# Embedding tower: the look-ups of each sub-block wait for the landing of the pair in front of them

## What is computed

```python
e = stack([tbl_f[ids[:, f]] for f in range(32)], axis=1)     # 1024 x 32 x 64
p, q = e[:, ROW], e[:, COL]                                  # 496 pairs of fields
z = sum(einsum('bpj,ipj->bpi', p, kernel) * q, axis=-1)      # 1024 x 496
h = relu(concat([z, dense_ctx]) @ W_top1 + b_top1)
y = relu(h @ W_top2 + b_top2) @ W_top3
```

## Time and profile before

| | us |
|---|---|
| median of 3 runs (495.70 to 498.19) | 495.96 |
| span of the profiled execution | 412.5 |
| outside the span, by the median | 83.5 |
| PE busy | 403.7 (98%) |
| DVE busy | 298.6 (72%) |
| ACT busy | 259.1 (63%) |
| POOL busy | 231.6 (56%) |

### The profile page before, as it was taken

How to read it: one execution, slowest core, us unless ns; L and a number is a source line. 1 busy time by engine, 2 the same in 40 slices (tenths; PEclk the granted TensorE clock), 3 DMA queues, 4 the chain that set the end, 5 groups by cost and what they waited for, 6 DMA issues and landing times.

```text
span 412.5 us, 10180 instructions
## 1 busy us (share of the span) xinstructions
PE 403.7 (98%) x3421; PEld 254.4 (62%) x3421; DVE 298.6 (72%) x293; ACT 259.1 (63%) x1874; POOL 231.6 (56%) x251
## 2 busy tenths in 40 slices
PE   7889999999999999999999999999999999999997
PEld 5556656667675766666766665666666566654442
DVE  6776887878788887878979798878879888740000
ACT  6476877667577876764796867719978667002221
POOL 6777777777677757776766777677767200000000
PEclk9998999999999999999999999999999999999999
DMA  6665661131281111211211113111311020000000
GB/s 177 210 200 155 191 221 33 27 77 27 37 219 28 29 19 47 61 28 25 63 42 28 25 25 79 24 27 26 79 25 27 15 51 2 2 2 0 2 0 1
DMA packets 18266, 24.31 MB, mean 59 GB/s; under 512 B 6387, under 2 KB 11767, under 8 KB 17958
## 3 DMA queue, kind: packets, MB, share of 16 engines
q1 hardware_dynamic: 10406, 15.64, 13.0%
q0 software_dynamic: 7808, 8.01, 9.7%
HBM read 19.44 MB, written 0.00 MB: 47 GB/s over the span
## 4 chain that ended last, share of the span: by engine, by line
PE 92%; DMA 3%; POOL 3%; issue 1%; ACT 0%
PE u_ps L690 41%; PE z_ps L724 14%; PE u_ps L711 13%; PE z_ps L730 7%; PE u_ps L771 7%; PE t_ps L644 4%; PE u_ps L791 3%; POOL nat L419 3%; DMA nat<-tbl,ids_sb 2%; PE u_ps L697 2%; DMA ids_sb<-ids 1%; PE t_ps L677 0%; PE u_ps L799 0%; ACT y_sb L571 0%
## 5 line engine op out<-in xcount | busy, mean ns | idle before, releaser
L419 POOL DMA_INDIRECT nat<-tbl,ids_sb x244 | 230.5, 945 | 90.7 <-issue 56.6
L607 DVE TENSOR_TENSOR prod<-u_ps,rows 128x1024 f32<-128x1024 f32 x184 | 213.5, 1218 | 56.7 <-PE u_ps L690 56.7
L504 ACT ACTIVATE pass_prod<-pass_prod 128x64 f32<-128x64 f32 x896 | 214.3, 243 | 22.1 <-DVE pass_prod L618 22.1
L690 PE MATMUL u_ps<-rows,k_sb 64*128 64x256 f32 x1472 | 176.2, 387 | 0.0
L504 ACT ACTIVATION_READ_ACCUMULATOR pass_prod<-pass_prod 128x1 f32 x896 | 169.9, 190 | 0.0
L690 PEld LDWEIGHTS u_ps<-rows,k_sb 64*128 64x128 f32 x1472 | 139.0, 188 | 46.0 <-DVE pass_prod L618 13.4
L618 DVE TENSOR_TENSOR pass_prod<-u_ps,nat 128x1024 f32<-128x1024 f32 x56 | 67.2, 1215 | 1.2 <-PE u_ps L711 1.2
L711 PE MATMUL u_ps<-k_sb,rows 64*128 64x256 f32 x448 | 61.5, 394 | 0.6 <-ACT rows L492 0.6
L724 PE MATMUL z_ps<-prod,sel 128*32 128x512 f32 x512 | 61.6, 598 | 0.0
L492 ACT ACTIVATE rows<-t_ps 128x512 f32<-128x512 f32 (+1 forms) x38 | 19.6, 516 | 54.2 <-PE t_ps L644 54.0
L711 PEld LDWEIGHTS u_ps<-k_sb,rows 64*128 64x128 f32 x448 | 40.6, 186 | 14.6 <-DVE prod L607 9.6
(11 more groups left out here) (50 smaller groups left out, 78.9 us busy)
## 6 DMA issues: line engine op xcount, KB each, us to landing
by_self<-rows SPq DMA_DIRECT2D x32, 128.0 KB
nat<-tbl,ids_sb POOLq DMA_INDIRECT x244
k_sb<-kern SPq DMA_DIRECT2D x3, 768.0 KB, 5.6
k_sb<-kern SPq DMA_DIRECT2D x2, 640.0 KB, 5.7
k_sb<-kern SPq DMA_DIRECT2D x1, 1152.0 KB, 5.2
k_sb<-kern SPq DMA_DIRECT2D x2, 512.0 KB
rows<-w SPq DMA_DIRECT2D x1, 1024.0 KB, 6.6
rows<-tbl SPq DMA_DIRECT2D x4, 224.0 KB
```

The costliest lines, as they stand in the source:

```text
L419: pool.indirect_dma_start(nat_of(m, n)[:, h * EMBED:(h + 1) * EMBED], None, tables[f], bass.IndirectOffsetOnAxis(ids_sb[:, col:col + 1], 0 ...
L504: op = nc.scalar.activation(of, of, ACT.Copy, accum_out=z_nat[:, b % 2, s, row:row + 1])
L607: nc.vector.tensor_tensor(to, u, by.unsqueeze(1).to_broadcast([P, 2, 2, SIZE]), ALU.mult).then_inc(prod_ready, 1)
L690: op = nc.tensor.matmul(u[:, h, :], k_sb[part, k_of(d), side, :], rows[part, tile, cols_of(b)], start=True, stop=True)
```

## The change

From tile m = 12 on POOL waits ahead of the first look-up of each sub-block. Ahead of sub-block 0 it waits until all four look-ups of tile m - 1 have landed; ahead of sub-block 1 until both look-ups of sub-block 0 of its own tile have landed. The second look-up of a sub-block follows without a new wait. So at most two look-ups are under way at any time, where before there was no such limit. The waits that were there stay, and no instruction of another engine changes.

```diff
+SPACED = 12
@@ the loop of POOL, for n in range(SUBS)
                 for n in range(SUBS):
+                    if m >= SPACED:
+                        if n == 0:
+                            pool.wait_ge(gathered[(m - 1) % LANES], lane_count(m - 1))
+                        else:
+                            pool.wait_ge(gathered[m % LANES], lane_count(m) - 32)
                     for h in range(2):
                         _, pieces, quads = PLAN.in_front(m, 2 * n + h)
```

## The result

The changed kernel is slower. In the comparison that followed the prediction it took 604.77 us (603.48 to 606.11, 4 runs) against 496.27 us (495.7 to 498.19, 4 runs), a ratio of 1.219 with the interval 1.214 to 1.223. The forecast was 629.5 us with a range of 600 to 656.

What follows compares the result with a forecast made beforehand. PE was taken as the bound; look-up pairs of 3.93 us would delay its last transposes by 131.8 us, and 1.7 us of reduced clock made 133.5 us. Added to 495.96 us this gave 629.5 us, range 600 to 656.

Steps and rivals of the forecast that it cites:

- The mechanism: From m = 16 on POOL's look-ups set the pace: 3.93 us for two instead of 2.64, PE idle about 5 us.
- The step of 1.25 us: On POOL, from first to second look-up issue in a sub-block: 1.25 us, as before, because nothing is waited for between them.
- The landing: From a pair's second look-up issue to its landing: 2.40 us, with 2.20 and 3.01 as ends.
- the case built on it: With a landing of 2.08 us a pair of look-ups takes 3.61 us and the time is near 596 us.
- The release of POOL: From a landing to POOL's next start: 0.28 us in each pair of look-ups, with 0.04 as low end.
- The large loads: Three look-up landings meet two `k_sb` loads and `w1` with `w2`: about 2 us each, 6 us in all.
- The sum: m = 63 lands at 464.4 us; PE's last transposes come 131.8 us later; with 1.7 us of clock, 133.5 us.
- The 83.5 us "outside the span": Time beyond the profiled span of 412.5 us, taken as unchanged and added to the forecast span of 546.0 us.
- The clock: PE runs at reduced clock after idle time; only after the last landing does this count: 1.7 us.
- the rival of the cold PE: Half clock stays on through PE's rounds, 10.7 us of work becomes 21.5; time about 765 us, chance 0.03.
- The waits cost nothing: Rival: look-up pairs with landing and release stay within PE's 2.72 us; time 496 us, chance 0.03.
- the low nor the high landing: Rivals: look-ups land after 2.20 us (584 us with 0.04 release) or 3.01 us (693 us); chance 0.06 each.

Runs made afterwards that it cites:

- after 2: The changed kernel, compared again with the kernel before, and its trace: 588.48 us, ratio 1.426.
- the later before: The kernel before, unchanged, timed again in the second comparison: 412.9 us over 7 runs.

## Why the prediction was right, point by point

*The mechanism.* Right. POOL's time for two look-ups became a closed chain, the lead was used up, and the look-ups set the pace. "About 24 times, some 5 us each", from m = 16 on, was 24 times 5.2 us. That PE waited at m = 13 and 15 already comes from two long steps of POOL at m = 12 and 13, told below.

*The step of 1.25 us* between the two look-ups of a sub-block: 1.24 to 1.25 us.

*The landing.* 2.40 us was taken between bounds of 2.20 and 3.01; it measured 2.40 for the last look-up and 2.45 in the median. Leaning to the low end because the DMA engines were quiet was right. The estimate of 2.08 us by the formula of the Trainium skill ("DMA: Bandwidth & Descriptors", section "Anatomy of one DMA — SWDGE (gpsimd) path") was 0.3 to 0.4 us short of it, and the case built on it, near 596 us, did not come about beside a before of the same speed.

*The release of POOL.* This is the term that was mis-sized. 0.28 us came from the only row in which POOL started on a landing, and it holds where the DMA carries the wait. It was applied to both waits. Ahead of sub-block 0 the landing is waited for by a separate instruction, and the release there is 0.75 us. That is 0.47 us more for each of 52 tiles, 24 us. The typical tile is 8.45 us and not 7.86, 31 us over 52 tiles; the 6 us that the release does not explain are landings a little above 2.40. The order listing in the front part shows the difference (`gathered4,transposed` against `gathered5` in the last place), but I had not read it as a price. The two kernels with the wait written first confirm the term.

*The large loads.* 6 us were taken. The distance from the landing of m = 11 at about 49.6 us to that of m = 63 at 504.7 is 455.1 us; 52 tiles of 8.45 are 439.4, so 15.7 us lie in single long steps. The three landings that the prediction named are there: 5.50 us at m = 12 and 6.27 at m = 13, beside the last `k_sb` loads, and 6.39 at m = 22, just behind the issue of `w1` and `w2` at 141.5 and 142.2 us. Against the usual steps they cost 9.5 us and not 6. The first of them in POOL's timeline of after 2:

```profile
51.57 0.94 POOL L425 DMA_INDIRECT nat<-tbl,ids_sb  x1 [0.30 <-issue]
57.07 0.94 POOL L425 DMA_INDIRECT nat<-tbl,ids_sb  x1 [4.56 <-DMA nat<-tbl,ids_sb]
```

The others cost about 6 us together, and only some lie beside a load. Two of them, 2.70 us at m = 31 and m = 53, are at the second look-up of sub-block 0, which waits for no landing. What these others are was not tested.

*The sum.* The landing of m = 63 was forecast at 464.4 us and came at 504.7: 31 us for the tile (24 of them the release) and 10 us for the long steps. Against a before of 412.9, the forecast loss of 133.5 us would have meant 546 us; measured were 588.5. So the loss was 24% too small.

*The time itself.* 604.8 us lay inside the range, but with luck. The loss was sized 42 us too small beside the later before, and it was put on top of a before of 496 us, 83 us above that one; the two errors partly cancel. The first comparison's own difference, 108.5 us, was below the 133.5 forecast, the later one, 175.6, above it. The 83.5 us "outside the span" were taken as a constant, which the runs of the changed kernel refute (1.8 us). The failed step is "with the 83.5 us outside the span unchanged". A gap of that size between time and span was a warning that the trace and the times were not of the same executions.

*The clock.* The direction was right and the place of its cost too. From the last transposes to the end it is 587.1 - 504.8 = 82.3 us. With only the wait ahead of sub-block 0, where PE did not wait at the last transposes, it is 505.1 - 425.25 = 79.9: 2.5 us for the cold start against 1.7 forecast. Inside a round that begins at half clock, as 17 of the 24 do by their transposes, it costs about 3 us and vanishes in the idle time, as foreseen. But the prediction took 10.7 us of work for every round, and PE's fixed order makes them uneven. Before, the round ahead of m = 32 held 7.1 us (161.18 to 168.28), and PE now stands 9.88 us behind it; the next one held 12.6 us, and with 3 us of cold start 1.28 us are left (264.77). Behind the round ahead of m = 60, 13.6 us before, it is 0.21 us. So the rival of the cold PE was near in single rounds, nearer than I had it. The section "Loop structure matters more than you think" of the Trainium skill's page "TensorE: Matmul & The Clock Gate" says that a long wait for DMA ahead of the matmuls lets PE run cold. The trace agrees, with the half clock behind 9.88 us of idle time and a mean clock of 0.78 to 0.86 by stretch.

*A reading.* "PE waited for look-ups 6 times, 7.6 us" adds PE's own 2 waits, 2.8 us, to 4 of its weight load, which overlaps it. Nothing in the sum uses it.

*The rivals.* "The waits cost nothing" is false for these waits: a landing would have had to come within 1.19 us of its issue. It is true for the same waits one pair later, where a landing may come 2.72 us later still, within 3.91 us, and takes 2.45 in the median. Neither the low nor the high landing, 2.20 and 3.01 us, was the usual one, and a cold PE without idle time did not come, since 125.6 us of idle time stand at its transposes.

## What to carry to other kernels

A wait for the landing of the transfer just issued turns an issue rate into a latency: 1.25 us for a look-up became 1.25 or 2.7 to 3.2. If transfers have to be spaced, wait for one that was issued long enough ago; one pair later the same 104 waits were free. The queue's busy share (0.69) says little about its slack, since its gaps of 0.30 us between two look-ups were never shorter in any of these traces. And before a sum is made on top of a median, the profiled span should lie close to it; a gap of 17% has to be explained first.

## What the runs showed of the hardware that was not expected

- On POOL, an indirect DMA starts 0.26 us after the semaphore that it carries itself, and 0.75 us after one that a separate wait instruction right in front of it waits for (after 2), or 0.79 us in the kernel with a wait ahead of every look-up. The steps are 2.69 to 2.72 against 3.20 to 3.24 us in the median, with the same landing of 2.42 to 2.45. Swapping two lines of waits was worth 29.4 us with 52 waits and 124 us with 208.
- A look-up of 128 rows of 256 bytes lands 2.42 us after the start of its instruction on POOL with one under way and 2.43 to 2.45 with two, in the median; single ones took up to 5.5 us.
- Half the clock after a stop of 4.18 us cost PE 2.5 us where it lay on the path.
